# The third layer's bias matmuls on 32 rows each, standing in pairs ahead of a unit's products

## The chip, the core and the metric

The kernel runs on one core of one Trainium2 chip. The core has five engines with queues of their own, which meet through semaphores: TensorE (PE in the profile, its weight loads apart as PEld), VectorE (DVE), ScalarE (ACT), GpSimd (POOL) and SyncE (SP), which only issues DMAs. The metric is the device time of one execution, in microseconds (us), given as the median of several runs.

## What is computed

Three layers of a graph network over 20000 nodes of 512 features and 5000 edges, in float32, with a last normalization of input plus result:

```python
def _sage_conv(h, src, dst, Wl, bl, Wr):
    msg = h[src]
    s = segment_sum(msg, dst, num_segments=N_NODES)
    cnt = segment_sum(ones((src.shape[0], 1)), dst, num_segments=N_NODES)
    agg = s / maximum(cnt, 1.0)
    return agg @ Wl.T + bl + h @ Wr.T

h, residual = x, 0.0
for Wl, bl, Wr, g, b in params:                 # three layers
    h = residual + _sage_conv(h, src, dst, Wl, bl, Wr)
    h = _layer_norm(h, g, b)
    h = _prelu(h, a_prelu)
    residual = h
return _layernorm(x + h)
```

The bias `bl` of a layer is a row of 512 numbers that is added to every node's row. It is the one thing whose handling in the third layer is changed.

## The kernel before

The 20000 nodes, sorted so that those with incoming edges come first, fill 157 tiles of 128 rows. A unit is two tiles (the last one of a layer has one), so a layer has 79 units, and the layers' units are numbered through. Twenty units of a layer are edge units: their tiles also need the mean of the incoming messages. In each layer 18 plain units come first, then twenty times an edge unit and two plain ones, then one plain unit. I number the units of the third layer 0 to 78 here; in it, the first run of plain units is 0 to 17.

TensorE's program (`tensor_program`) does three things with a unit, in the order of the loop at its end. `turn` transposes the next unit's rows, eight 128x128 transposes into `ps_t` (L355). `sum_messages` (L367) multiplies messages by a matrix of matches, for edge units only. `product_self` and `product_mean` make the products of a tile: `mm3` (L374) writes 12 matmuls of 128x512 per tile into one bank of `ps_z`, a float32 product made of three products of high and low parts (`w_hi`, `w_lo`, `hT_hi`, `hT_lo`). An edge unit has 24 more of them.

In layers one and two, VectorE adds the bias on top of the products. In the third layer TensorE does that itself: the first matmul into a tile's bank, at L392, has `ones_full` (128x128 ones) as its weights and `bias_full` (128x512) as its moving operand. Row 0 of `bias_full` is the high part of the centred bias, row 1 is its low part, and the other 126 rows are zero, so the matmul writes the bias into all 128 rows of the bank. `mm3` then adds to it. So a third-layer unit has two bias matmuls, each ahead of its own tile's 12 products.

There are two `ps_z` buffers, of two banks each, used by units in turn. So unit u may write into its banks only when VectorE has read unit u-2 out of them, at L762 (`normal`), which counts the semaphore `gained` once per tile. The first bias matmul waits for tile 0 of unit u-2, the second for tile 1. A unit's products also wait for its low part at L744 (`take_low`, semaphore `low`), and so do the transposes of the following unit, since `ps_t` is read there. On VectorE, `take_low` of unit u stands directly ahead of `normal` of unit u-2. VectorE further does the prelu at L767 and the third layer's sum with x at L809; ScalarE the high parts (L476) and squares (L488, L529); GpSimd the roots (L632, L644), the shift at L638 and the scattered stores at L655.

The operands of the bias matmul are made once, before the first unit: the bias is loaded into `bias_raw` (two rows), centred and rounded by ScalarE (L468, L471, L553), and the low part is put into row 1 by VectorE at L884. VectorE zeroes the rest at L817.

Of the kernel before, what the change touches and what calls it, by code (L numbers as in the profile page):

```python
# [6 lines left out]

P = 128
ALU = mybir.AluOpType
ACT = mybir.ActivationFunctionType  # L10
# [5 lines left out]
L = 3  # L16
# [12 lines left out]
def build_program(nc, x, wT, bl, g, b, a_prelu, ident_in, const_in, edge_cols_in, edge_last_in, edge_rows_in,  # L29
# [50 lines left out]
    with ExitStack() as ctx:  # L80
        def sb(name, shape, dt=F32, where=ctx):
            return where.enter_context(nc.sbuf_tensor(name, shape, dt))
# [16 lines left out]
        bias_rows = sb("bias_rows", [P, L - 1, D])  # L99
        bias_full = sb("bias_full", [P, D], F32R)  # L100
        bias_raw = sb("bias_raw", [2, D])
        bias_neg = sb("bias_neg", [P, L])
        row_select = sb("row_select", [2, 1])
        ones_full = sb("ones_full", [P, P], F32R)
# [8 lines left out]
        y = [sb(f"y{i}", [P, 2, D]) for i in range(2)]  # L113
        hout = [sb(f"hout{i}", [P, 2, D]) for i in range(3)]
        junk = [sb(f"junk{i}", [P, D]) for i in range(2)]
        ssq = [sb(f"ssq{i}", [P, 2]) for i in range(2)]
# [127 lines left out]
        def sync_program(sp):  # L244
# [62 lines left out]
            for l in range(L - 1):  # L307
                sp.dma_start(bias_rows[:, l, :], spread(bl[l], P)).then_inc(bias_in, 16)
            sp.dma_start(bias_raw[:], spread(bl[L - 1], 2)).then_inc(bias_in, 16)
            sp.dma_start(row_select[:], row_select_in).then_inc(bias_in, 16)  # L310
# [25 lines left out]
        def tensor_program(pe):  # L336
# [42 lines left out]
            def product_self(u, j):  # L379
                if j >= u.n:  # L380
                    return
                if j == 0:
                    pe.wait_ge(low, u.no + 1)
                    if u.pos == 0:
                        pe.wait_ge(w_low, KC * (2 * u.l + 1))
                        if u.l == L - 1:
                            pe.wait_ge(bias_done, 1)
                reach(pe, gained, Unit(u.no - 2).ahead + j + 1 if u.no >= 2 else 0)
                acc = ps_z[u.r2][:, j, :]
                own_bias = u.l == L - 1  # L390
                if own_bias:
                    pe.matmul(acc, ones_full[:], bias_full[:], start=True, stop=False)  # L392
                mm = mm3(acc, hT_hi[u.r2][:, j], hT_lo[u.r2][:, j], 2 * u.l, not own_bias, not u.edge)
                if not u.edge:
                    mm.then_inc(z_ready, 1)
# [55 lines left out]
        def scalar_program(act):  # L451
# [13 lines left out]
            def center_bias(l):  # L465
                rows_ = bias_rows[:, l, :] if l < L - 1 else bias_raw[:]
                mean = bias_neg[:, l:l + 1] if l < L - 1 else bias_neg[0:2, l:l + 1]
                nc.scalar.activation(junk[0][:] if l < L - 1 else junk[0][0:2, :], rows_, ACT.Identity, scale=-1.0 / D,  # L468
                                     accum_out=mean).then_inc(bias_mean, 1)
# [82 lines left out]
            act.wait_ge(ready, 1)  # L552
            nc.scalar.copy(bias_full[0:2, :], bias_raw[:]).then_inc(bias_high, 1)  # L553

# [143 lines left out]
        def vector_program(dve):  # L698
# [117 lines left out]
            nc.vector.memset(eps[:], EPS)  # L816
            nc.vector.memset(bias_full[:].bitcast(F32), 0.0)  # L817
            nc.vector.memset(ones_full[:].bitcast(F32), 1.0).then_inc(ready, 1)
# [33 lines left out]
            for c in range(KC):  # L852
# [30 lines left out]
            nc.vector.tensor_scalar(slope_less[:], slope[:], -1.0, 1.0, ALU.mult, ALU.add)  # L883
            nc.vector.scalar_tensor_tensor(bias_full[0:2, :], bias_full[0:2, :].bitcast(F32), row_select[:],  # L884
                                           bias_raw[:], ALU.mult, ALU.add).then_inc(bias_done, 1)
            dve.wait_ge(bias_done, 1)
# [110 lines left out]
```

## Time and profile before

| what | us |
|---|---|
| median of 3 runs | 2153.39 (2153.33 to 2155.93) |
| the profiled execution, own time | 2155.8 |
| its span, first to last instruction | 2154.0 |
| TensorE busy | 2052.4 (95%) |
| VectorE busy | 1748.0 (81%) |
| GpSimd busy | 1506.4 (70%) |
| ScalarE busy | 1194.4 (55%) |

The profile is one execution. Matmuls are pipelined: a 128x512 matmul is shown with about 400 ns, but the next begins about 233 ns after it began, so the distance between starts, not the length of a row, is what a matmul costs. An engine's busy time says little on what bounds a stretch; the chain of waits, followed back from the last instruction, and the starts within a unit say it. The third layer runs from about 1413 us to the end.

### The profile page before, as it was taken

To read this page: it belongs to the slowest core of one execution; us is meant where nothing else is said; L and a number is where in the kernel's file an instruction comes from. 1 tells how busy PE (TensorE), PEld (TensorE's weight loads), DVE (VectorE), ACT (ScalarE), POOL (GpSimd) and SP (SyncE) were. 2 spreads that over 40 slices of the span, in tenths; PEclk is the share of its full clock that TensorE was granted. 3 is DMA by queue.
4 is the path that set the end of the run, shared out by engine and by line. 5 is a ranking of instruction groups with operands and counts; after the bars stand their busy time and mean duration, and the time that the engine had idled before them with its cause. 6 is when DMAs were issued, how large, how long until landed. Compare 5 with 4: busy or idle time off the path is not lost.

```text
span 2154.0 us, 31040 instructions
## 1 busy us (share of the span) xinstructions
PE 2052.4 (95%) x10342; PEld 1693.0 (79%) x10342; DVE 1748.0 (81%) x2656; ACT 1194.4 (55%) x2485; POOL 1506.4 (70%) x1198
## 2 busy tenths in 40 slices
PE   6778999999999999999999999999999999999991
PEld 4566888888888878888888888888788888888881
DVE  7558798899987688777777777789889999899992
ACT  3434455445444455444444444458877777777775
POOL 2886788888876556555555555468888888788876
PEclk8989999999999999999999999999999999999996
DMA  5346666676666545444444444355655555555542
GB/s 178 135 139 207 225 202 225 220 226 209 209 210 207 176 162 177 150 147 147 147 149 149 149 149 149 124 191 195 214 210 200 192 197 198 188 204 196 189 156 99
DMA packets 180943, 387.46 MB, mean 180 GB/s; under 512 B 20108, under 2 KB 20553, under 8 KB 180783
## 3 DMA queue, kind: packets, MB, share of 16 engines
q1 hardware_dynamic: 142222, 271.80, 36.6%
q0 software_dynamic: 38560, 113.67, 15.8%
q8 instruction: 83, 1.36, 0.2%
q14 instruction: 78, 0.63, 0.1%
HBM read 220.81 MB, written 164.79 MB: 179 GB/s over the span
## 4 chain that ended last, share of the span: by engine, by line
PE 82%; POOL 8%; DVE 4%; issue 4%; ACT 1%; DMA 0%; POOLq 0%; SPq 0%; ACTq 0%; DVEq 0%
PE ps_z L374 67%; PE ps_t L355 8%; PE ps_s L367 5%; POOL y L638 3%; POOL node_found L679 2%; DVE y L762 1%; POOL out L655 1%; PE ps_z L392 1%; POOL rstd L632 1%; DVE o_sb L809 1%; POOL hin L603 1%; POOL orstd L644 1%; DVE hout L767 0%; DVE sumT L716 0%; ACT hT_hi L476 0%
## 5 line engine op out<-in xcount | busy, mean ns | idle before, releaser
L374 PE MATMUL ps_z<-w_hi,hT_hi 128*128 128x512 f32 x1884 | 766.8, 407 | 1.5 <-DVE y L762 1.5
L374 PE MATMUL ps_z<-w_lo,hT_hi 128*128 128x512 f32 x1884 | 750.0, 398 | 0.0
L374 PE MATMUL ps_z<-w_hi,hT_lo 128*128 128x512 f32 x1884 | 747.2, 397 | 0.0
L488 ACT ACTIVATE junk<-ps_z 128x512 f32<-128x512 f32 x471 | 280.8, 596 | 781.7 <-DVE ps_z L754 633.5
L638 POOL TENSOR_TENSOR y<-y,shift 128x1024 f32<-128x1024 f32 (+1 forms) x237 | 573.5, 2420 | 188.6 <-DVE y L762 185.5
L767 DVE SCALAR_TENSOR_TENSOR hout<-hout,slope_less,y 128x1024 f32<-128x1024 f32 (+1 forms) x237 | 427.7, 1804 | 3.6 <-ACT hout L503 3.6
L374 PEld LDWEIGHTS ps_z<-w_hi,hT_lo 128*128 128x128 f32 x1884 | 356.8, 189 | 86.6
L374 PEld LDWEIGHTS ps_z<-w_lo,hT_hi 128*128 128x128 f32 x1884 | 357.6, 190 | 76.3
L374 PEld LDWEIGHTS ps_z<-w_hi,hT_hi 128*128 128x128 f32 x1884 | 358.2, 190 | 75.3 <-DVE y L762 2.0
L632 POOL TENSOR_TENSOR rstd<-veps,minus_half 128x2 f32<-128x2 f32 (+1 forms) x237 | 249.4, 1052 | 238.7 <-ACT veps L494 237.9
L754 DVE TENSOR_TENSOR ps_z<-ps_z,bias_rows 128x512 f32<-128x512 f32 x314 | 215.1, 695 | 211.3 <-PE ps_z L374 202.3
L762 DVE SCALAR_TENSOR_TENSOR y<-ps_z,rstd,gain 128x512 f32<-128x512 f32 x471 | 329.6, 740 | 50.4 <-POOL rstd L632 50.4
L744 DVE TENSOR_TENSOR hT_lo<-ps_t,hT_hi 128x1024 fp32r<-128x1024 f32 (+1 forms) x237 | 287.1, 1211 | 94.4 <-ACT hT_hi L476 86.4
L503 ACT ACTIVATE hout<-y 128x1024 f32<-128x1024 f32 (+1 forms) x237 | 249.9, 1054 | 72.0 <-POOL y L638 69.6
L355 PEld LDWEIGHTS ps_t<-ident,hin 128*128 128x128 f32 x1884 | 221.1, 141 | 40.9 <-issue 10.2
L355 PE MATMUL ps_t<-ident,hin 128*128 128x128 f32 x1884 | 246.9, 274 | 6.1 <-DVE hT_lo L744 6.0
L476 ACT CAST hT_hi<-ps_t 128x1024 fp32r<-128x1024 f32 (+1 forms) x237 | 234.7, 990 | 17.9 <-issue 13.3
L655 POOL DMA_INDIRECT out<-o_sb,node_put x157 | 187.0, 1191 | 63.0 <-issue 61.5
L809 DVE SCALAR_TENSOR_TENSOR o_sb<-hout,o_sb 128x512 f32<-128x512 f32 x157 | 218.7, 1430 | 8.8
L603 POOL DMA_INDIRECT hin<-in_x,node_get x157 | 158.4, 1009 | 68.2 <-issue 35.3
L374 PE MATMUL ps_z<-w_hi,sT_hi 128*128 128x512 f32 x480 | 190.3, 396 | 0.9 <-DVE sT_lo L801 0.9
L374 PE MATMUL ps_z<-w_lo,sT_hi 128*128 128x512 f32 x480 | 189.9, 396 | 0.0
(127 smaller groups left out, 2213.0 us busy)
## 6 DMA issues: line engine op xcount, KB each, us to landing
h_scratch<-hout SPq DMA_DIRECT2D x156, 512.0 KB
hin<-h_scratch SPq DMA_DIRECT2D x156, 512.0 KB
x_by_slot<-hin SPq DMA_DIRECT2D x78, 512.0 KB
o_sb<-x_by_slot SPq DMA_DIRECT2D x78, 512.0 KB, 3.7
rowtab<-edge_row_table SPq DMA_DIRECT2D x60, 256.0 KB
stage<-in_WrT SPq DMA_DIRECT2D x3, 1024.0 KB
stage<-in_WlT SPq DMA_DIRECT2D x3, 1024.0 KB
hin<-in_x,node_get POOLq DMA_INDIRECT x157
```

Of the source, the lines that this page charges most:

```text
L355: mm = pe.transpose(ps_t[:, j, k * P:(k + 1) * P], hin[u.r3][:, j, k * P:(k + 1) * P], ident[:])
L374: mm = pe.matmul(acc, a[:, k, :], ww[:, k, :], start=start, stop=stop and k == KC - 1 and a is a_lo)
L476: nc.scalar.copy(hT_hi[u.r2][:, 0:u.n].rearrange("p j k n -> p (j k n)"), ps_t[:, 0:u.n, :].rearrange("p j d -> p (j d)")).then_inc(high, 1)
L488: nc.scalar.activation(junk[j][:], ps_z[u.r2][:, j, :], ACT.Square, accum_out=ssq[u.r2][:, j:j + 1]).then_inc(squared, 1)
L503: nc.scalar.activation(hout[u.r3][:, 0:u.n, :], y[u.r2][:, 0:u.n, :], ACT.Relu, scale=-1.0).then_inc(parted, 1)
L632: nc.gpsimd.tensor_tensor(rstd[u.r2][:, 0:u.n], veps[u.r2][:, 0:u.n], minus_half[:, 0:u.n], ALU.pow).then_inc(rstd_done, 1)
L638: nc.gpsimd.tensor_tensor(y[u.r2][:, 0:u.n, :], y[u.r2][:, 0:u.n, :], moved, ALU.add).then_inc(shifted, 1)
L744: nc.vector.tensor_tensor(hT_lo[u.r2][:, 0:u.n].rearrange("p j k n -> p (j k n)"), ps_t[:, 0:u.n, :].rearrange("p j d -> p (j d)"), hT_hi[ ...
L754: nc.vector.tensor_tensor(acc, acc, bias_rows[:, u.l, :], ALU.add).then_inc(biased, 1)
L762: nc.vector.scalar_tensor_tensor(y[u.r2][:, j, :], ps_z[u.r2][:, j, :], rstd[u.r2][:, j:j + 1], gain[:, u.l, :], ALU.mult, ALU.mult).then_ ...
L767: nc.vector.scalar_tensor_tensor(hout[u.r3][:, 0:u.n, :], hout[u.r3][:, 0:u.n, :], slope_less[:, 0:1], y[u.r2][:, 0:u.n, :], ALU.mult, ALU ...
L809: nc.vector.scalar_tensor_tensor(o_sb[u.ring][:, j, :], hout[u.r3][:, j, :], 1.0, o_sb[u.ring][:, j, :], ALU.mult, ALU.add, accum_out=osum ...
```

## The change

Two bias matmuls of a unit get 32 rows of the array each and go next to each other. Tile 0's takes partitions 0 to 31 of its operands, tile 1's takes partitions 32 to 63, and both are issued ahead of tile 0's products. The wait on `gained` ahead of tile 0 is now for both tiles of unit u-2; the wait ahead of tile 1 is gone. In the built program the two matmuls have array tiles of 32 rows by 128 columns at rows 0 and 32; all others of the main loop have 128 by 128.

The operands follow: `bias_full` has 64 rows (twice the same 32, of which two hold numbers), and the weights are `ones_rows`, ones in the two rows that count and zeros in the other 30. The memset of `bias_full` is gone, one VectorE instruction that makes `ones_rows` is added, and the raw bias is loaded and centred on 64 rows instead of two, in room of `hout[2]`, which is not yet in use then.

```diff
-        bias_full = sb("bias_full", [P, D], F32R)
-        bias_raw = sb("bias_raw", [2, D])
+        bias_full = sb("bias_full", [2 * Q, D], F32R)
-        row_select = sb("row_select", [2, 1])
+        row_select = sb("row_select", [Q * 2, 2])
+        ones_rows = sb("ones_rows", [Q * 2, P], F32R)
...
+        bias_raw = hout[2][0:2 * Q, 0, :]
...
-            sp.dma_start(bias_raw[:], spread(bl[L - 1], 2)).then_inc(bias_in, 16)
+            sp.dma_start(bias_raw, spread(bl[L - 1], 2 * Q)).then_inc(bias_in, 16)
...
-                reach(pe, gained, Unit(u.no - 2).ahead + j + 1 if u.no >= 2 else 0)
                 acc = ps_z[u.r2][:, j, :]
                 own_bias = u.l == L - 1
-                if own_bias:
-                    pe.matmul(acc, ones_full[:], bias_full[:], start=True, stop=False)
+                if own_bias and j == 0:
+
+                    pe.wait_ge(gained, Unit(u.no - 2).upto)
+                    for jj in range(u.n):
+                        at = slice(Q * jj, Q * (jj + 1))
+                        pe.matmul(ps_z[u.r2][:, jj, :], ones_rows[at, :], bias_full[at, :], start=True, stop=False)
+                elif not own_bias:
+                    reach(pe, gained, Unit(u.no - 2).ahead + j + 1 if u.no >= 2 else 0)
...
-            nc.vector.memset(bias_full[:].bitcast(F32), 0.0)
...
-            nc.vector.scalar_tensor_tensor(bias_full[0:2, :], bias_full[0:2, :].bitcast(F32), row_select[:],
-                                           bias_raw[:], ALU.mult, ALU.add).then_inc(bias_done, 1)
+            nc.vector.tensor_scalar(ones_rows[:], ones_full[0:2 * Q, :].bitcast(F32), row_select[:, 1:2], None, ALU.mult)
+            nc.vector.scalar_tensor_tensor(bias_full[0:2 * Q, :], bias_full[0:2 * Q, :].bitcast(F32), row_select[:, 0:1],
+                                           bias_raw, ALU.mult, ALU.add).then_inc(bias_done, 1)
```

What this moves, on TensorE, at a plain unit near the start of the third layer. `ps_t` takes the transposes, `ps_z1` is the unit's pair of banks. Before:

```order
L355 MATMUL ps_t<-ident,hin1 128x128 [waits low,h_in1]
L355 MATMUL ps_t<-ident,hin1 128x128 x7
L392 MATMUL ps_z1<-bias_full,ones_full 128x512 [waits gained,low]
L374 MATMUL ps_z1<-w_hi4,hT_hi1 128x512
L374 MATMUL ps_z1<-w_lo4,hT_hi1 128x512
...
L374 MATMUL ps_z1<-w_hi4,hT_lo1 128x512
L392 MATMUL ps_z1<-bias_full,ones_full 128x512 [waits gained]
L374 MATMUL ps_z1<-w_hi4,hT_hi1 128x512
```

And now (the lines have moved by a few numbers):

```order
L357 MATMUL ps_t<-ident,hin1 128x128 [waits low,h_in1]
L357 MATMUL ps_t<-ident,hin1 128x128 x7
L397 MATMUL ps_z1<-bias_full,ones_rows 128x512 [waits gained,low]
L397 MATMUL ps_z1<-bias_full,ones_rows 128x512
L376 MATMUL ps_z1<-w_hi4,hT_hi1 128x512
L376 MATMUL ps_z1<-w_lo4,hT_hi1 128x512
```

The number of matmuls is the same. The second one has moved from between the two tiles' products to directly behind the first, its wait is merged into the first one's, and no other engine's loop has changed.

## Rows read from the trace of the kernel before

**Rows 1.** Page, part 1 and two lines of part 2.

```profile
PE 2052.4 (95%) x10342; PEld 1693.0 (79%) x10342; DVE 1748.0 (81%) x2656; ACT 1194.4 (55%) x2485; POOL 1506.4 (70%) x1198
...
PEclk8989999999999999999999999999999999999996
```

**Rows 2.** Chain that ended last, 1413 to 1545: start us, length us, what.

```profile
1432.57 3.13 DVE o_sb L809 x3
...
1506.72 2.43 POOL y L638
```

**Rows 3.** The same chain, 1540 to 2100.

```profile
1551.14 5.85 PE ps_z L374 x24
1556.99 0.87 PE ps_t L355 x8
1557.86 0.23 PE ps_z L392
...
2052.14 0.87 PE ps_t L355 x8
...
2080.35 0.87 PE ps_t L355 x8
...
2092.94 0.03 ACT junk L488
...
2099.48 2.41 POOL y L638
```

**Rows 4.** Timeline of PE in a plain unit: start us, length us, engine, what.

```profile
1600.67 1.03 PE L355 MATMUL ps_t<-ident,hin 128*128 128x128 f32 x8
1601.47 0.48 PE L392 MATMUL ps_z<-bias_full,ones_full 128*128 128x512 f32 x1
1601.78 0.40 PE L374 MATMUL ps_z<-w_hi,hT_hi 128*128 128x512 f32 x1
...
1604.35 0.39 PE L374 MATMUL ps_z<-w_hi,hT_lo 128*128 128x512 f32 x1
1604.58 0.40 PE L392 MATMUL ps_z<-bias_full,ones_full 128*128 128x512 f32 x1
1604.82 0.40 PE L374 MATMUL ps_z<-w_hi,hT_hi 128*128 128x512 f32 x1
```

**Rows 5.** Timeline of PEld, the weight loads of the same unit.

```profile
1601.44 0.19 PEld L392 LDWEIGHTS ps_z<-bias_full,ones_full 128*128 128x128 f32 x1
1601.55 0.19 PEld L374 LDWEIGHTS ps_z<-w_hi,hT_hi 128*128 128x128 f32 x1
1601.78 0.19 PEld L374 LDWEIGHTS ps_z<-w_lo,hT_hi 128*128 128x128 f32 x1
```

**Rows 6.** Line L355 from 1544 to 2106: duration ns min/median/max.

```profile
L355 PE MATMUL ps_t<-ident,hin x470: 270/272/273, 1543.8 to 2100.0; 128*128 128x128 f32 x157
```

**Rows 7.** Timelines around 30.8 us: a transpose of one row, then full ones.

```profile
30.82 0.19 PE L425 MATMUL ps_z<-ident,runs_ahead 1*40 1x1 f32 x1 [0.39 <-DVE runs_ahead L869]
...
30.93 1.35 PEld L355 LDWEIGHTS ps_t<-ident,hin 128*128 128x128 f32 x7
```

**Rows 8.** Around 198.9 us: line L407, and the loads behind it.

```profile
L407 PE MATMUL ps_s<-ident,table x2: 272/300/328, 198.7 to 198.9; 128*128 128x128 f32 x1, 128*29 128x128 f32 x1
...
198.88 0.25 PEld L355 LDWEIGHTS ps_t<-ident,hin 128*128 128x128 f32 x2
...
198.99 0.30 PE L355 MATMUL ps_t<-ident,hin 128*128 128x128 f32 x1
```

**Rows 9.** Timeline of VectorE ahead of the unit of rows 4.

```profile
1596.69 1.41 DVE L762 SCALAR_TENSOR_TENSOR y<-ps_z,rstd,gain 128x512 f32<-128x512 f32 x2
```

**Rows 10.** Timelines of PE and VectorE in one of units 12 to 16.

```profile
1503.50 1.06 PE L355 MATMUL ps_t<-ident,hin 128*128 128x128 f32 x8 [0.40 <-DVE hT_lo L744]
1504.32 0.48 PE L392 MATMUL ps_z<-bias_full,ones_full 128*128 128x512 f32 x1
...
1511.02 0.85 PE L355 MATMUL ps_t<-ident,hin 128*128 128x128 f32 x6 [0.41 <-DVE hT_lo L744]
...
1503.27 1.40 DVE L762 SCALAR_TENSOR_TENSOR y<-ps_z,rstd,gain 128x512 f32<-128x512 f32 x2
```

**Rows 11.** Who waited for whom, 1544 to 2107: us in total, times, longest.

```profile
DVE hT_lo L744 <- ACT hT_hi L476: 38.1, 22, 3.9
```

**Rows 12.** Timeline before the first unit, VectorE.

```profile
33.80 0.15 DVE L883 TENSOR_SCALAR slope_less<-slope 128x1 f32<-128x1 f32 x1
33.88 0.73 DVE L884 SCALAR_TENSOR_TENSOR bias_full<-bias_full,row_select,bias_raw 2x512 fp32r<-2x512 f32 x1
```

More of the change, by code:

```diff
@@ L8 @@
 P = 128
+Q = 32
 ALU = mybir.AluOpType
@@ L465, in center_bias @@
             def center_bias(l):
-                rows_ = bias_rows[:, l, :] if l < L - 1 else bias_raw[:]
-                mean = bias_neg[:, l:l + 1] if l < L - 1 else bias_neg[0:2, l:l + 1]
-                nc.scalar.activation(junk[0][:] if l < L - 1 else junk[0][0:2, :], rows_, ACT.Identity, scale=-1.0 / D,
+                rows_ = bias_rows[:, l, :] if l < L - 1 else bias_raw
+                mean = bias_neg[:, l:l + 1] if l < L - 1 else bias_neg[0:2 * Q, l:l + 1]
+                nc.scalar.activation(junk[0][:] if l < L - 1 else junk[0][0:2 * Q, :], rows_, ACT.Identity, scale=-1.0 / D,
                                      accum_out=mean).then_inc(bias_mean, 1)
@@ L552, in scalar_program @@
             act.wait_ge(ready, 1)
-            nc.scalar.copy(bias_full[0:2, :], bias_raw[:]).then_inc(bias_high, 1)
+            nc.scalar.copy(bias_full[0:2 * Q, :], bias_raw).then_inc(bias_high, 1)
             for T in range(-1, UNITS + 5):
@@ L989 @@
     ident = given("ident", np.eye(P, dtype=np.float32))
-    row_select = given("row_select", np.array([[0.0], [-1.0]], np.float32))
+    row_select = given("row_select", np.array([[-(r % Q == 1), r % Q < 2] for r in range(2 * Q)], np.float32))
     out = nc.dram_tensor("out", x.shape, F32, kind="ExternalOutput").ap()
```

## The prediction

> **What bounds the kernel now.** I read the page's first two parts, then the chain that ended last, then single units in the timelines. TensorE is busy for 95% of the span, and its granted clock is nine tenths of full speed or more in all slices but three, two at the start and the last; in the third layer up to its end it is the full 2.4 GHz level [rows 1], so costs read there hold there. The share alone doesn't say where it is the bound, and only the third layer, from 1413 us on, is touched. The chain splits that layer in three. Up to about 1551 us the chain runs over VectorE's L809 and GpSimd's L638 and not over TensorE [rows 2]. From 1551.14 us, in the last products of the first edge unit, it stays on TensorE until the ScalarE square at 2092.94 us, and it then goes over to GpSimd for the rest [rows 3]. In the middle piece nothing lies between TensorE's instructions, and one period (an edge unit and two plain units) is 2080.35 - 2052.14 = 28.21 us [rows 3]. From the transposes at 1556.99 to the end of the piece at 2092.9 that is 535.9 / 28.21 = 19.0 periods of three units, so **57 units, each with two bias matmuls**, stand where TensorE's time is the kernel's time. The other 22 units of the layer are elsewhere.
>
> **What a bias matmul costs.** The second of a unit begins at 1604.58 and the product behind it at 1604.82, after one that begins 0.23 us before: 0.234 us in the chain, like any 128x512 matmul, with its weights loaded under the one before [rows 4]. The first of a unit stands behind the transposes, which are spaced at 0.109 us (0.87 / 8, rows 3). Its weight load begins at 1601.44, the next load at 1601.55, so **a load holds the load path for 0.11 us**, and the first product begins at 1601.78, 0.23 us behind that second load [rows 5]. The load after a matmul thus begins when that matmul really starts; the matmul's row is drawn early and long (0.48 us) because it waits for its weights.
>
> **What the change does to a pair.** Removed: 2 x 0.234 = 0.467 us of TensorE per unit. Added: two matmuls on different rows of the array, writing to different banks. No row of this trace has two matmuls running side by side, so I bound it. The dear end is no overlap: 0.467 us, gain nothing. The cheap end is a full overlap of both loads and both matmuls: 0.234 us, gain 0.234 us. Between them is what rows 5 suggest: the two matmuls stream together, but the second load follows the first, 0.11 us later, and isn't hidden, since both stand behind short transposes and there is no long matmul to hide it. Then the second matmul starts 0.11 us behind the first and the pair takes 0.109 + 0.234 = 0.343 us; the gain is **0.125 us per unit**. I take this value, since the spacing of loads is the row nearest to the case. Over 57 units: 0.125 x 57 = 7.1 us (the cheap end: 0.234 x 57 = 13.3 us).
>
> The Trainium skill, page "TensorE: Matmul & The Clock Gate", section "Part 3: Packing small matmuls — row/col tiling", says that matmuls on different row groups start about 4 ns apart. By it the pair would cost about what one matmul costs, which is the cheap end above. No row here shows it.
>
> **What changing the array's tile costs.** The two matmuls use array tiles of 32 rows, the transposes ahead of them and the products behind them 128, so a unit has two changes of tile. The trace has two places with one. At 30.82 us a transpose of one row (a tile of 32 rows) begins, and the first load for a full one begins at 30.93, 0.11 us later and before the first one's row ends at 31.01; this at half clock and behind a wait, so 0.11 us is a bound from above for one change and much of it is issue [rows 7]. At 198.88 us a 128*29 transpose (the same rows, fewer columns) begins, the next full load begins at 198.88 too, and the next full transpose at 198.99: the usual 0.11 us, so a change of columns cost nothing [rows 8]. I take 0 for a change, and keep 0.11 as the end for the forecast's range and for a rival below. The products behind the pair wait for nothing new: what they read, `low` has released already.
>
> **The wait moved forward.** The pair waits for both tiles of unit u-2. In the middle piece VectorE's two L762 end at 1596.69 + 1.41 = 1598.10, 3.3 us ahead of the bias matmul at 1601.47 [rows 4, 9]; the wait costs nothing in all 57 units. In units 12 to 16 and 18 it does bind: the two L762 end at 1504.67, 0.35 us after the bias matmul begins at 1504.32 [rows 10], so the pair starts some 0.4 us late. Behind it are queued the unit's products and then the next transposes. But there TensorE has slack: it waits 0.4 us for `low` ahead of the transposes, and its own work from 1503.50 to its next transposes is about 6.93 us (0.87 + 26 x 0.233) of the 1511.02 - 1503.50 = 7.52 us [rows 10], 0.59 us free. 0.4 us late less 0.125 us saved fits. Whoever waits for the products (ScalarE's squares) comes to them later still, as the chain is not on TensorE there. So price and gain are 0 in those units, and also in units 0 to 17 as a whole: what TensorE saves there it waits for VectorE and GpSimd [rows 2]. In the last three units the chain is on GpSimd, gain 0 [rows 3].
>
> **The rest.** VectorE loses a memset near the start and gets one short instruction before the first unit: L883, of its kind, takes 0.15 us and L884 keeps its 0.73 us, since 64 rows take what two take for the same 512 elements [rows 12]. It may shift the start by 0.15 us; I leave it to the range. The raw bias is one DMA as before. No queue is passed by anything: SP, POOL and ACT keep their orders.
>
> **Is the next bound far?** With 0.125 us per unit a period becomes 28.21 - 0.375 = 27.84 us. VectorE waits 38.1 us for ScalarE's high parts between 1544 and 2107 [rows 11], which wait for TensorE's transposes; over 20 periods that is 1.9 us each, more than the 0.375 us, and more than the 0.70 us of the cheap end. So it passes through.
>
> **Sum.** Against the profiled execution's own 2155.8 us: 2155.8 - 7.1 = 2148.7. That execution was 2.4 us above the median of 2153.39, and the gain holds for both, so the forecast is 2153.4 - 7.1 = **2146.3 us**. Its own range is 2143 to 2150 (a change of tile costing up to 0.05 us on one side, loads partly side by side on the other).
>
> **Rivals.** (a) *Both loads and matmuls fully side by side*: 2153.4 - 13.3 = 2140.1 us. For: different rows of the array have their own weights. Against: in rows 5 loads come one at a time. (b) *The change doesn't do what it says*: the matmuls run one after the other, or each change of tile eats half of the gain (0.06 us twice), 0 in sum: 2153.4 us. (c) *Each change of tile empties the array, and the load behind it is no longer hidden*; this is the one that ends slower. It decides from 0.125 us for both changes together. By rows 7 each costs up to 0.11 us, so 0.22 - 0.125 = 0.095 us per unit, x 57 = +5.4 us, **2158.8 us**. If the next load really waits for the end that the rows draw, it is dearer: 0.272 - 0.109 = 0.16 us behind the transposes [rows 6], and behind the pair 0.40 + 0.11 - 0.234 = 0.27 us, since the load of the first product begins only when the second bias matmul's 0.40 us row has ended [rows 4, 5]. That is 0.43 - 0.125 = 0.31 us per unit, x 57 = +17.4, 2170.8 us. Against the dear form: in rows 7 the load begins before the row of the matmul ahead has ended, and in rows 8 under the matmul.
>
> The Trainium skill, page "TensorEngine Tiling (Array Packing)", section "Key Properties", says that changing the tiling mode, not just the tile, drains TensorE, and gives no time. By that rule the time is rival (c)'s, 2158.8 to 2170.8 us; rows 8 don't show it for columns, and no row shows it under a 512-column matmul.
>
> **How the numbers follow.** The forecast 0.34, (a) 0.19, (b) 0.19, (c) 0.28. A measurement of this kernel can tell about 0.2% (4.3 us) from no change, so the forecast and (a) count as faster: 0.53; (b) is within: 0.19; (c) is slower: 0.28. Since cases of both signs hold weight, the range goes from (a)'s 2140.1, a little lower for some gain in the first units, 2139, up to 2168, which leaves out only the dearest end of (c); the likeliest case's own range is 2143 to 2150.
>
> **What the profile after would show.** Right: in the middle piece the bias matmuls' starts about 0.11 us apart, the first product 0.34 us behind the first one's real start, a period near 27.84 us, and units 0 to 18 at their old places. For (a) starts a few ns apart and a period near 27.5; for (b) 28.2 unchanged. For (c) a gap ahead of the first bias load, and the load of the first product starting only behind the pair, with a period of 28.5 to 29.1 us. The forecast is wrong if the granted clock falls in the layer, if the wait on `gained` shows up outside units 12 to 18, or if the gain of a period is given back by VectorE.

## The result

| | before | after |
|---|---|---|
| median, us | 2153.71 (2153.33 to 2155.93, 6 runs) | 2163.4 (2162.84 to 2164.08, 6 runs) |
| ratio, 95% interval | 1 | 1.0043 [1.0032, 1.0053] |
| span of the profiled execution | 2154.0 | 2161.3 |

The change makes the kernel 9.7 us slower, where 7.1 us faster were forecast. The profiled execution of before was 2.1 us above this median, so the two spans differ by less than the medians do. The time lies in the middle piece of the third layer. Before, it ran from 1551.14 to 2092.94 us, 541.8 us [rows 3]. After, the chain that ended last has it here (start us, length us, what):

```profile
1549.84 5.86 PE ps_z L376 x24
1555.70 0.87 PE ps_t L357 x8
1556.58 0.42 PE ps_z L397
...
1564.57 0.42 PE ps_z L397
1564.99 3.01 PE ps_z L376 x12
1568.00 0.89 PE ps_s L369 x8
1568.89 2.81 PE ps_z L376 x12
...
2059.38 0.87 PE ps_t L357 x8
...
2088.07 0.87 PE ps_t L357 x8
...
2100.79 0.02 issue
```

From 1549.84 to 2100.79 it is 551.0 us, 9.2 more. A period (an edge unit and two plain ones) is 2088.07 - 2059.38 = **28.69 us**, 0.48 more than the 28.21 of before [rows 3], or 0.16 us per unit. The shape shows where: the pair stands in the chain with 0.42 us, where a single bias matmul had 0.23 [rows 3], and the 12 products behind it take 3.01 us, while the second tile's, with no bias in front, take 2.81. So behind the pair another 0.20 us is lost.

The timeline of one plain unit of after, first PE, then PEld (start us, length us, engine, what, and in brackets idle time ahead of it), against rows 4 and 5:

```profile
1612.94 1.03 PE L357 MATMUL ps_t<-ident,hin 128*128 128x128 f32 x8
1613.90 0.50 PE L397 MATMUL ps_z<-bias_full,ones_rows 32*128 32x512 f32 x2
1614.33 0.50 PE L376 MATMUL ps_z<-w_hi,hT_hi 128*128 128x512 f32 x1
1614.67 0.39 PE L376 MATMUL ps_z<-w_lo,hT_hi 128*128 128x512 f32 x1
```

```profile
1613.90 0.18 PEld L397 LDWEIGHTS ps_z<-bias_full,ones_rows 32*128 32x128 f32 x2 [0.17 <-issue]
1614.33 0.19 PEld L376 LDWEIGHTS ps_z<-w_hi,hT_hi 128*128 128x128 f32 x1 [0.25 <-issue]
1614.44 0.19 PEld L376 LDWEIGHTS ps_z<-w_lo,hT_hi 128*128 128x128 f32 x1
1614.67 0.19 PEld L376 LDWEIGHTS ps_z<-w_hi,hT_lo 128*128 128x128 f32 x1
```

Four things are to be seen. The two bias matmuls share one row of 0.50 us, and one of them alone is recorded with this:

```profile
L397 PE MATMUL ps_z<-bias_full,ones_rows x114: 489/492/497, 1556.5 to 2088.9; 32*128 32x512 f32 x114
```

Two that take 0.49 us each end 0.50 us after the first one's start, so they run **fully side by side**: in the single records both their starts and their loads are 3 ns apart. Second, the load path stands idle ahead of the pair: the loads begin 0.20 us after the start of the last transpose, where before they began at it. Third, it stands idle behind the pair: the next load begins at 1614.33, 0.43 us after the pair, where a 512-column matmul lets the next load begin at once. Fourth, the load behind that begins at 1614.44, which is when the first product really starts: the product's own 0.11 us load is no longer under anything. The wait for VectorE that was moved forward is hardly to be seen. In the third layer, once each in units 0, 16 and 17 (us in total, times, longest):

```profile
PE ps_z L397 <- DVE y L769: 1.4, 3, 0.9
```

**The account of a unit**, from the start P of the last transpose: before, the first product starts at P + 0.343, and the other bias matmul costs 0.234 later, 0.577 in all. After, it starts at P + 0.201 + 0.427 + 0.109 = P + 0.737, and nothing more comes. The difference is 0.16 us, x 57 units = 9.1 us, against 9.2 us in the chain.

### The profile page after: what moved, and what is told of

It is laid out like the page before. It is cut to its first block, busy times and chain, and to the rows that moved or that the text cites. A ratio compares the mean times of both kernels' runs of the same rounds, so it can differ in the third digit from the quotient of the medians.

```text
span 2161.3 us, 31040 instructions
## 1 busy us (share of the span) xinstructions
PE 2060.7 (95%) x10342; PEld 1679.1 (78%) x10342; DVE 1751.2 (81%) x2656; ACT 1194.0 (55%) x2485; POOL 1505.1 (70%) x1198
## 4 chain that ended last, share of the span: by engine, by line
PE 84%; POOL 8%; issue 4%; DVE 3%; ACT 1%; DMA 0%; POOLq 0%; SPq 0%; ACTq 0%; DVEq 0%
PE ps_z L376 69%; PE ps_t L357 8%; PE ps_s L369 5%; POOL y L645 3%; POOL node_found L686 2%; POOL out L662 1%; PE ps_z L397 1%; DVE y L769 1%; POOL rstd L639 1%; POOL hin L610 1%; POOL orstd L651 1%; DVE sumT L723 0%; PE ps_s L344 0%; ACT hT_hi L483 0%; DVE ps_z L761 0%
## 5 line engine op out<-in xcount | busy, mean ns | idle before, releaser
L376 PE MATMUL ps_z<-w_hi,hT_hi 128*128 128x512 f32 x1884 | 775.7, 412 | 1.5 <-DVE y L769 1.5
```

The costliest lines, as they stand in the source:

```text
L376: mm = pe.matmul(acc, a[:, k, :], ww[:, k, :], start=start, stop=stop and k == KC - 1 and a is a_lo)
```

## The experiments

Two things were to be told apart first: whether the loss is the change of array tile (theory T), or the new order with its merged wait (rival W); then how much of the pair's overlap is real, what sets the price of a change, and where the bias would cost least. Except for the first one, and where it is said, edits are shown against the kernel after. Each ratio is to executions of before taken together with that run, whose medians lie between 2153.1 and 2154.4 us. In the stretches that the periods are taken from, TensorE's granted clock is 1.00 in every run, the 2.4 GHz level. The period is always between the transposes of the same two units, 16 periods apart, over 16.

| run | median, us | ratio to before | period, us |
|---|---|---|---|
| before | 2153.7 | 1 | 28.21 |
| after | 2163.4 | 1.0043 | 28.69 |
| e1 together, 128 rows | 2154.3 | 1.0003 [0.9993, 1.0013] | 28.23 |
| e2 apart, 32 rows | 2207.9 | 1.0254 [1.0237, 1.0271] | 30.53 |
| e3 pair on the same rows | 2178.3 | 1.0114 [1.0097, 1.0131] | 29.38 |
| e4 pair, 64 rows | 2163.5 | 1.0045 [1.0028, 1.0062] | 28.70 |
| e6 no bias | 2127.0 | 0.9872 [0.9857, 0.9887] | 26.82 |
| e7 pair ahead of the transposes | 2164.8, one run | | 28.55 |
| e9 transpose of 29 columns | 2159.9, one run | | 28.52 |
| e8 ScalarE writes the bias | 2154.3 | 0.9998 [0.9989, 1.0008] | 28.07 |
| e10 only in the unit behind an edge unit | 2145.3 | 0.9963 [0.9949, 0.9977] | 27.74 |
| e11 in both plain units | 2141.2 | 0.9946 [0.9933, 0.996] | 27.31 |
| e12 in all three | 2138.7 | 0.993 [0.9914, 0.9945] | 27.30 |
| e13 as e12, tensors placed anew | 2132.6 | 0.9907 [0.9891, 0.9924] | 27.85 |

### Together, on 128 rows

The order and the merged wait of after, with the operands of before; against the kernel before:

```diff
-                reach(pe, gained, Unit(u.no - 2).ahead + j + 1 if u.no >= 2 else 0)
...
-                if own_bias:
-                    pe.matmul(acc, ones_full[:], bias_full[:], start=True, stop=False)
+                if own_bias and j == 0:
+                    pe.wait_ge(gained, Unit(u.no - 2).upto)
+                    for jj in range(u.n):
+                        pe.matmul(ps_z[u.r2][:, jj, :], ones_full[:], bias_full[:], start=True, stop=False)
```

> The kernel before with the two bias matmuls of a unit together in front and one wait for both tiles, as in the changed kernel, but on all 128 rows: order and wait alone, without the change of array tile. Theory T (what costs is the change from 128-row to 32-row array tiles and back): no change, 2153.7 us, period of an edge unit and two plain ones 28.2 us, pair 0.47 us. Rival W (the wait that was moved forward and the new order cost the time): 9.7 us slower, about 2163 us, period 28.7 us.

Measured: 2154.3 us, no change, and the period of before. W falls: order and wait cost nothing that the medians can tell (0.6 us between them), and the period is 28.23 us where W had 28.7.

### Apart, on 32 rows

The reverse, the order of before with the 32-row operands:

```diff
+                reach(pe, gained, Unit(u.no - 2).ahead + j + 1 if u.no >= 2 else 0)
+                if own_bias:
+                    at = slice(Q * j, Q * (j + 1))
+                    pe.matmul(acc, ones_rows[at, :], bias_full[at, :], start=True, stop=False)
```

> The changed kernel with its 32-row matmuls put back to their old places, one ahead of each tile's products, with the old waits. Theory T: each place pays for leaving and re-entering the 128-row tile, +0.39 us against a hidden 128-row matmul by the rows of the changed kernel, so 2 x 0.39 = 0.78 us per unit, 57 units: +44 us and some more in units 0 to 17, 2195 to 2203 us; a period of 28.21 + 2.35 = 30.6 us. If only the pairing and the wait cost (W): 2153.7 us.

Measured: 2207.9 us, the period longer than that of before by 2.33 us, 0.77 per unit, 0.39 per place with its change there and back. The place between two products, timelines of PE and PEld:

```profile
1615.64 0.40 PE L376 MATMUL ps_z<-w_hi,hT_lo 128*128 128x512 f32 x1
1615.97 0.49 PE L395 MATMUL ps_z<-bias_full,ones_rows 32*128 32x512 f32 x1
1616.39 0.50 PE L376 MATMUL ps_z<-w_hi,hT_hi 128*128 128x512 f32 x1
```

```profile
1615.96 0.18 PEld L395 LDWEIGHTS ps_z<-bias_full,ones_rows 32*128 32x128 f32 x1 [0.37 <-issue]
1616.39 0.19 PEld L376 LDWEIGHTS ps_z<-w_hi,hT_hi 128*128 128x128 f32 x1 [0.24 <-issue]
1616.49 0.19 PEld L376 LDWEIGHTS ps_z<-w_lo,hT_hi 128*128 128x128 f32 x1
```

The load of the 32-row matmul waits until 0.33 us after the start of the product ahead, and the next full load until 0.43 us after the bias matmul's start. So T holds, and the price belongs to the change of tile, wherever it stands: one matmul that runs alone pays as much behind it as a pair does. The time came out higher than expected since some 10 us are also lost in units 0 to 18 (144.7 us from the first transposes of unit 0 to those of unit 19, before 135.0). The prediction had TensorE with room in all of units 0 to 17; it has 0.59 us a unit near the end of that run alone [rows 10], where the units' transposes start 7.5 us apart. From those of unit 3 to those of unit 12 they start 6.93 us apart in before, which is TensorE's own work, and 7.70 us apart here, so there TensorE sets the pace and all of the 0.77 us is lost.

### The pair on the same rows

```diff
-                        at = slice(Q * jj, Q * (jj + 1))
+                        at = slice(0, Q)
```

> The changed kernel with both matmuls of a pair on rows 0 to 31: the changes of tile stay, the running side by side is taken away. Theory T with a real overlap of 0.234 us: 0.392 us per unit over before, 57 units: +22 us, 2176 us, second bias matmul 0.23 us behind the first, period 29.4 us. If the overlap in the trace were only drawn, and both run one after the other already: 2163.4 us as the changed kernel.

Measured: 2178.3 us, period 29.38. PE's row of the pair, and the first product's:

```profile
1617.14 0.73 PE L397 MATMUL ps_z<-bias_full,ones_rows 32*128 32x512 f32 x2
1617.80 0.50 PE L376 MATMUL ps_z<-w_hi,hT_hi 128*128 128x512 f32 x1
```

On the same rows the pair takes 0.73 us instead of 0.50, and a period is 0.69 us longer: 0.23 per unit. The second load starts 0.11 us after the first, as between full-row matmuls, so a 32-row matmul behind another one pays nothing extra: the price is that of the change, not of having fewer rows. That 0.23 us is what the overlap is worth, the whole of a matmul. So the pair brings what rival (a) said and the changes of tile cost what (c) said: -0.23 + 0.39 = +0.16. The median is some 2 us above the expected 2176, as part of the 0.39 us a unit is also lost in the first run of plain units.

### The pair on 64 rows each

```diff
-Q = 32
+Q = 64
```

> The changed kernel with 64 rows each (array tiles of 64 rows, at rows 0 and 64) instead of 32. Theory T, if any other tile than the 128-row one costs the same: 2163 us, period 28.7 us. If the cost goes with how small the tile is: between 2153.7 and 2163 us.

Measured: 2163.5 us, period 28.70, the same as on 32 rows. Between these two, the size of the tile doesn't matter.

### No bias in the third layer

The third layer's two bias matmuls are left out, and with them the bias; the first product starts each bank.

> The kernel before without the third layer's bias matmuls: that layer's bias is left out of the result. It measures what the two bias matmuls are worth on the path. If TensorE alone is the bound in 57 units and nothing is close behind: 57 x 0.467 = 26.6 us faster, 2127 us, period 28.21 - 1.40 = 26.81 us. If VectorE (waiting only 1.9 us a period before) or GpSimd takes over: less, 2130 to 2145 us.

Measured: 2127.0 us. Both bias matmuls are worth 27 us, and the next bound is not close behind: a period falls by 1.39 us, 0.46 per unit, which is two matmuls. This is as far down as any treatment of the bias can go by TensorE's time, as long as its products keep their pace.

### The pair ahead of the transposes

A unit's products stand behind the transposes of the following unit. Here the pair is issued ahead of those transposes instead of behind them, so that it is entered from a product and left into a transpose. In the loop of `tensor_program`:

```diff
+                if u.exists and u.l == L - 1:
+                    pe.wait_ge(gained, Unit(u.no - 2).upto)
...
+                    for jj in range(u.n):
+                        at = slice(Q * jj, Q * (jj + 1))
+                        pe.matmul(ps_z[u.r2][:, jj, :], ones_rows[at, :], bias_full[at, :], start=True, stop=False)
                 if ahead.exists:
                     turn(ahead)
```

> The changed kernel with the 32-row pair moved ahead of the next unit's transposes: it is now entered from a 512-column product and left into a transpose. If each change of tile empties the array whatever stands around it: load of the pair 0.32 us after the last product's start (as in the runs with 32-row matmuls ahead of each tile), next load 0.43 us after the pair's, together again 0.16 us per unit over the kernel before, period 28.7 us. If the neighbours matter (the short transposes were what made it dear): period 28.2 us or less. In units 0 to 18 the earlier wait for both tiles of unit u-2 holds up the transposes, so its total may be some us above 2163.

Measured: 2164.8 us in one run, period 28.55, so 0.11 us a unit above before, where 0.16 or nothing was expected. The place, from PE's timeline:

```profile
1653.17 0.40 PE L376 MATMUL ps_z<-w_hi,hT_lo 128*128 128x512 f32 x1
1653.50 0.49 PE L436 MATMUL ps_z<-bias_full,ones_rows 32*128 32x512 f32 x2
1653.93 0.65 PE L357 MATMUL ps_t<-ident,hin 128*128 128x128 f32 x4
```

The load ahead of the pair starts 0.33 us after the last product (behind a transpose it was 0.20), which is 0.09 above the spacing of products, as 0.20 was 0.09 above that of transposes. The next load follows 0.43 us behind the pair's, as before. What is better by 0.05 us a unit is the load that is no longer hidden: that of a transpose holds the load path for 0.057 us there, that of a product for 0.108. The rest stays, so neither place makes the pair pay. The total is above that of after because the moved wait binds in units 0 to 18, which take 142.1 us in this trace against 135.8 in after. TensorE waits 5.6 us for VectorE's L770 there, and soon after the two longest of these waits, 1.7 us up to 1411.90 and 1.9 us up to 1537.74, the granted clock is 0.50 for 3.4 us, from 1413.0 and from 1539.3. One run doesn't tell the medians apart; the period does.

### A change of columns

Against the kernel before: one full transpose of each third-layer unit's second tile is done twice, the first time with 29 columns only (array tile 128x32), between full ones.

```diff
+                        if u.l == L - 1 and j == 1 and k == KC - 1:
+                            pe.transpose(ps_t[0:29, j, k * P:(k + 1) * P], hin[u.r3][:, j, k * P:k * P + 29], ident[:])
```

> The kernel before with one more transpose per third-layer unit of two tiles, of 29 columns of weights on all 128 rows (array tile 128 by 32), ahead of the unit's last transpose, which overwrites it. It is the case of the rows around 198.9 us. If a change of columns alone costs nothing, as those rows read: 0.05 to 0.11 us per unit, period 28.4 to 28.5 us, 2157 to 2160 us. If it empties the array as a change of rows does: 0.2 us or more twice per unit, period at least 29.4 us.

Measured: period 28.52, 0.10 us per unit more, which is one more transpose and nothing else. PEld around it:

```profile
1612.55 0.11 PEld L356 LDWEIGHTS ps_t<-ident,hin 128*29 128x29 f32 x1
1612.66 0.14 PEld L357 LDWEIGHTS ps_t<-ident,hin 128*128 128x128 f32 x1
1612.77 0.19 PEld L394 LDWEIGHTS ps_z<-bias_full,ones_full 128*128 128x128 f32 x1
```

Every load follows at 0.11 us. So what rows 8 showed was true, and true of columns only; it said nothing on a change of rows. The one run's 2159.9 us is 5.5 us above the median of before taken with it; 57 x 0.104 is 5.9.

### ScalarE writes the bias into the banks

If the bias matmuls are worth 27 us, they may go to an engine with room. ScalarE, busy for 55% of the span, copies the bias row into both banks of a unit, and all of TensorE's products accumulate onto it; there is no bias matmul.

```diff
+            def fill_bias(u):
+                act.wait_ge(gained, Unit(u.no - 2).upto)
+                nc.scalar.copy(ps_z[u.r2][:, 0:u.n, :],
+                               bias_rows[:, L - 1:L, :].to_broadcast([P, u.n, D])).then_inc(filled, 1)
```

> A version that takes the third layer's bias off TensorE without a change of tile: ScalarE writes the bias into both banks of a unit (one 128x1024 copy, about 1.05 us by its like at L503) once unit u-2 has been read, and all products accumulate onto it. If TensorE is the bound and ScalarE has the room (434 of 562 us busy in the middle piece, 8.3 of 9.4 us a unit with the copy): up to 26.6 us faster, 2127 to 2135 us. If ScalarE, in order, delays the high parts or squares: 2140 us or no gain, most of all in units 0 to 17, where it is busy 44.3 of 52 us.

Measured: 2154.3 us, as before, but this total adds up two things: the kernel reached the third layer some 12 us earlier, for a reason that stands in "The place of the operands", and lost as much in it. Who waits for the fill, from 1544 to 2100 us:

```profile
PE ps_z L370 <- ACT ps_z L472: 23.5, 21, 1.5
```

The fill takes 1.01 us and comes late in ScalarE's order. TensorE waits about 1.3 us for it in an edge unit, 0.1 to 0.3 us in the unit ahead of one and not at all in the unit behind one; and some 12 us go in units 0 to 17 (136.7 us against 125.1), where ScalarE has little room. Not all of that is waiting. Behind a wait of 2.5 us for the fill, up to 1403.54, the granted clock is 0.50 from 1404.9 for 3.4 us, and near the end of one of 2.9 us, up to 1446.54, it falls at 1445.8 for 6.8 us; TensorE is busy for 9.5 of these 10.2 us, at half its pace. A period, which is taken at full clock, fell by only 0.14 us, although six bias matmuls are gone from it and its products with `hT` are quicker. By stretches the place decides, so the next three fill only where there is room.

### Only where there is room

The fill only in the unit behind each edge unit (e10); then in both plain units (e11); then in all units behind the first edge unit but the layer's last two, and issued earlier in ScalarE's order (e12). The units that aren't filled keep the two matmuls of before. `FILLED` is (1,) in e10, (1, 2) in e11 and (0, 1, 2) in e12; `LEAD` is the 18 plain units that come first, `UL` the 79 units of a layer, so 0 stands for edge units and 1 and 2 for the plain ones behind them. Against the kernel before:

```diff
+FILLED = (1,)
...
+            self.filled = self.l == L - 1 and LEAD < self.pos < UL - 2 and (self.pos - LEAD) % 3 in FILLED
```

> The kernel before, but in the middle piece ScalarE writes the bias into the banks of one unit in three, the plain one right behind an edge unit; the others keep their 128-row bias matmuls. In the run in which ScalarE did it for all units this was the unit for which TensorE did not wait (its fill ended 1.8 us ahead). If the room of ScalarE is the limit there: 0.467 us for each of 19 units, 8.9 us faster, 2145 us, period 27.74 us. If one fill already shifts ScalarE's squares and high parts enough: 2149 to 2153 us.

> The same for both plain units of a period; edge units and the first 19 units of the layer keep their bias matmuls. ScalarE's room allows it by its busy time (434 of 562 us, 38 fills of 1.05 us more). If it has the room at the right time: 17.7 us faster, 2136 us, period 27.27 us. If the second unit's fill comes late, as it did by 0.25 us in the run with all units filled: about 2140 to 2145 us.

> All three units of a period are filled by ScalarE, with the copy ahead of the square of the current unit's first tile instead of behind it; the first 19 units keep their bias matmuls. If the late fill was a matter of order alone: period 26.8 us, 2128 to 2132 us. If ScalarE is full over two plain units in a row: TensorE still waits for the edge unit's fill, period 27.5 to 28.1 us, 2140 to 2153 us.

Measured: 2145.3, 2141.2 and 2138.7 us. Of the first two, each takes what two matmuls cost off a period, 0.47 and 0.43 us. The second came out 5 us above the better of its two expected times all the same. Its period is the expected one; about 4 us are lost once, between the transposes of units 21 and 22, which start 12.57 us apart where it is 8.72 in e10. TensorE waits 2.5 us for the fill of unit 20 there, since ScalarE has waited 2.3 us for GpSimd (L650, L659) ahead of it, and from 1566.0 the granted clock is 0.50 for 3.4 us: the 12 products behind the wait take 4.58 us in the chain instead of 2.80. In e12 the wait at this place is 1.95 us, and the clock stays at 1.00. The third brings little more in the period, since TensorE then waits for fills again (1560 to 2080 us):

```profile
PE ps_z L375 <- ACT ps_z L481: 4.8, 7, 2.0
```

### The place of the operands

One thing in the kernel in which ScalarE fills all units was not expected: it reached the third layer 10 to 13 us earlier than every other (first transposes at 1395.7 us against 1405.8 to 1408.5), though nothing in the first two layers' loop was changed. Its products with `hT` followed each other at 0.227 us (median, layers two and three) instead of 0.232 to 0.235. It was the only one without `row_select`, and so its tensors lay elsewhere in SBUF (their addresses are those of the built program; a tensor takes a multiple of 32 bytes of each partition). Against e12:

```diff
-        row_select = sb("row_select", [2, 1])
...
+        gap_a = sb("gap_a", [P, 16])
         sumT = [sb(f"sumT{i}", [P, KC, P]) for i in range(2)]
         sT_hi = [sb(f"sT_hi{i}", [P, KC, P], F32R) for i in range(2)]
         sT_lo = [sb(f"sT_lo{i}", [P, KC, P], F32R) for i in range(2)]
+        row_select = sb("row_select", [2, 1])
+        gap_b = sb("gap_b", [P, 16])
```

> The kernel in which ScalarE fills all units early (2138.7 us), with nothing changed but where tensors lie in SBUF. In every kernel but the two without row_select (a tensor of two numbers that takes a slot of 32 bytes), hT_hi and hT_lo begin 32 bytes behind a multiple of 64 bytes. The kernel in which ScalarE first filled the bias had them at multiples of 128 bytes, and its products with hT stood 0.227 us apart in layers 2 and 3 against 0.232 to 0.235 elsewhere, while its products with sT (64 bytes behind a multiple of 128) stayed at 0.233. Here row_select moves behind sT_lo, and two gaps of 64 bytes put hT, sT and the weights of all three layers at multiples of 128 bytes. Theory P (the place of the operands sets the pitch): all products 0.227 us apart; 24 products a unit and 48 in an edge unit save some 0.006 each, 0.15 us a plain and 0.3 us an edge unit, in the third layer a period of about 26.7 instead of 27.30, and over three layers of about 75 units 30 to 36 us, so 2101 to 2112 us. If 64 bytes were enough for hT and sT has another cause, sT stays at 0.233 and the time is some 3 us more. Rival Q (it was something else in that kernel, such as the 2 KB less ahead of hT or ScalarE's writes): pitches as in the kernel it is made from, 2138.7 us, within 0.2%.

Measured: 2132.6 us. The placing is the cause for `hT`: in all three layers its products are 0.227 us apart. The chain in the second layer, this kernel and then e12, a plain unit each (start us, length us, what):

```profile
850.67 5.48 PE ps_z L377 x24
```

```profile
853.23 5.59 PE ps_z L375 x24
```

The third layer begins 16.3 us earlier than in e12 (1390.9 against 1407.2). The products with `sT` went only from 0.234 to 0.232 or 0.233, so most of what sets their pace is something else. And only 6.1 of the 16.3 us are left at the end: the period is 27.85 us against 27.30, and TensorE waits three times as long for the fills (1560 to 2050 us):

```profile
PE ps_z L377 <- ACT ps_z L483: 15.1, 31, 1.1
```

The shares of the chain that ended last, 1600 to 2050 us, say that TensorE is no longer the bound there; first e12, then e13:

```profile
by line: PE ps_z L375 63.2%; issue 7.3%; PE ps_t L356 6.5%; PE ps_s L368 4.4%; POOL rstd L644 2.7%; POOL y L650 2.7%; POOL orstd L656 2.3%; POOL msg L638 1.7%; ACT stage L540 1.6%; POOL out L667 1.6%; ACT junk L499 1.5%; ACT o_sb L554 1.5%;
```

```profile
by line: issue 25.3%; POOL y L652 15.5%; POOL out L669 9.1%; POOL rstd L646 8.5%; POOL msg L640 8.4%; POOL orstd L658 8.2%; PE ps_z L377 5.0%; ACT junk L501 4.2%; ACT sT_hi L526 3.7%; ACT stage L542 3.3%; ACT o_sb L556 3.1%; POOL omove L661
```

In e12 70% of it is TensorE's products and transposes; in e13 the chain goes over GpSimd, with a quarter of it between instructions. Why GpSimd's round takes 27.9 us here, when it kept up with 27.3 in e12, stays open. Its records, rough as they are on this engine, show where: from 1600 to 2050 us a scattered store (L669, six a period) takes 1.21 us on the mean against 1.10, a gather (L640, two a period) 1.26 against 1.04, together about 1.1 us a period. It is the fastest kernel of all, 0.93% below before and 1.4% below after.

## Why the prediction was wrong

- **Where the kernel is bound: right.** In the middle piece, with its 57 units, all that TensorE loses reaches the end. The chain gives +9.2 us there, and 57 x 0.16 is 9.1. The reason for counting nothing in units 0 to 17 holds in part: from the transposes of unit 3 to those of unit 12 TensorE sets the pace too (6.93 us apart before, 7.10 after), and this loss is made up for only because the units behind had 0.59 us each to spare. At 0.16 us a unit that is enough, and units 0 to 18 take 135.8 us after against 135.0; at 0.77 us (e2) it is not.
- **The cost of a bias matmul, 0.234 us: right.** Without both, a period falls by 1.39 us, 0.46 per unit.
- **"Then the second matmul starts 0.11 us behind the first and the pair takes 0.109 + 0.234 = 0.343 us": mis-sized.** The spacing of loads in rows 5 is that of loads into the same rows. Loads into different rows start 3 ns apart and the matmuls as well, and e3 prices the overlap at 0.23 us, where the prediction had 0.125. The Trainium skill, page "TensorE: Matmul & The Clock Gate", section "Part 3: Packing small matmuls — row/col tiling", gives about 4 ns between the starts. After's trace agrees, with 3 ns.
- **"I take 0 for a change, and keep 0.11 as the end": this is the step that failed.** A change of the array's rows there and back costs 0.39 us: 0.20 in (0.201 from the last transpose to the pair's loads, before 0.002), 0.19 out (0.427 + 0.109 until the product really starts, less the 0.234 and 0.109 that a matmul and its hidden load take). The forecast with both terms right is -0.234 + 0.39 = +0.16 us per unit, 57 units, 2153.4 + 9 = 2162.4 us; 2163.4 was measured. The two rows behind the 0 couldn't carry it. Rows 8 have a change of columns, which costs nothing (e9), not of rows. Rows 7 have a change of rows, but with one column, at half clock and behind a wait of 0.39 us, so there was hardly any work in the array whose end a load could have waited for; "a bound from above" was wrong, since it doesn't bound the case of full work on both sides. What TensorE waits for inside a change is not recorded. The records show that ahead of the pair the load path stands idle until 0.09 us past the usual spacing, and that behind it the next load begins only after 0.43 us.
- **Rival (c) named the mechanism.** Its two signs were seen, the gap ahead of the first bias load and the product's load only behind the pair. Its dear form had the out-going load wait for the end of the row, 0.40 us; it begins 0.43 us after the start, with a row of 0.49. Its time of 2158.8 to 2170.8 holds the result, and so does the range, but in part by luck: both ends count the overlap at 0.125 us. With the 0.234 us that was measured, its prices of 0.22 and 0.43 us give 2152.6 and 2164.6 us, so only its dear form comes near. The Trainium skill, page "TensorEngine Tiling (Array Packing)", section "Key Properties", says that a changed tiling mode drains TensorE. The traces agree for a change of rows, with 0.20 us into the mode and 0.19 us out of it; for a change of columns alone, 128x128 to 128x32, e9 shows nothing of it, and there the measurement decides.
- **The wait moved forward: right.** e1, which has just that, shows no difference. After waits 1.4 us for it in all, in units 0, 16 and 17, where the prediction had units 12 to 16 and 18. The 0.3 us in unit 0 lie outside the units that it named as a sign, and cost nothing that can be seen at the end.
- **The rest, 0: right** as far as can be told; the new VectorE instruction ahead of the first unit leaves no trace in the later times.

## What to carry over

A matmul on part of the array's rows is not judged by its own time but by its two neighbours: here the way in and out costs 0.39 us with full-row work on both sides, more than the 0.23 us that running two 512-column matmuls side by side saves, so by these numbers it takes at least three side by side to gain, which no run tried. When a price is taken as 0 from a row that shows something similar, ask in what it differs (columns for rows, one column for 512, an idle engine for a full one), and if the remaining case decides the sign, give it the larger chance. What the two bias matmuls really cost was seen by leaving them out (27 us), and the better answer was to move them to another engine where it has room, which took some 15 us.

## What the runs showed of the hardware that wasn't expected

- A change of the array's rows costs alike for 32 and 64 rows (28.69 and 28.70 us per period), alike behind transposes and between products (0.39 us there and back), and a change of columns costs nothing (0.10 us for an extra transpose). It is the change that costs: a second 32-row matmul on the same rows has its load 0.11 us behind the first one's and costs 0.23 us more, like a full-row one (e3).
- Two weight loads into different rows of the array go at the same time (3 ns apart); into the same rows they are 0.11 us apart (e3).
- Where the operands lie in SBUF changes the pace of products: with `hT` at a multiple of 128 bytes and the weights `w` too, 128x512 matmuls follow each other at 0.227 us, with `hT` 32 bytes behind one at 0.232 to 0.235. In the kernel e8, `hT` was at such a multiple, but the first layer's weights were 32 bytes short of one, and there the first layer's products kept 0.230 to 0.238 us; in e13 both were placed and they went to 0.227, so by these two runs both operands count. A tensor of two numbers declared ahead of them was what shifted `hT`, and placing everything anew was worth 16 us over two layers. Whether 64 bytes would do wasn't tried, why a place matters isn't shown by any run, and why `sT` gains next to nothing is open.
- A long wait of TensorE in a busy stretch costs more than itself. At or just behind single waits of 1.7 to 2.9 us the granted clock fell to 0.50, the 1.2 GHz level, for 3.4 or 6.8 us (e7 twice, e8 three times, e11 once); at one of 1.95 us in e12 it didn't.
